# A Mamba mixer, cross attention and experts on one core: Delta's store, the load of B and C, w, the split of the products by C, and the order of the pieces

## The reference, cut to what matters

```python
h = conv(xc) + conv_b;  u = silu(h)                # 512 inner channels, 3 taps
dlt, Bm, Cm = split(u @ W_x.T)                     # 64, 16, 16
delta = softplus(dlt @ W_dt.T + b_dt)
dA  = exp(einsum('bld,dn->bldn', delta, -exp(A_log)))
dBu = einsum('bld,bln,bld->bldn', delta, Bm, u)
# scan in chunks of 64 tokens, the state starts at zero in each:
carry = dA * carry + dBu;  y = einsum('bkdn,bkn->bkd', carry, C)
y = y * silu(res);  out = y @ W_out.T + b_out
```

## Time and profile before

| | us |
|---|---|
| median of 3 runs (2793.26 to 2803.66) | 2795.64 |
| the profiled execution | 2792.28 |
| its span | 2790.5 |
| busy: PE | 2424.6 (87%) |
| busy: DVE | 2140.0 (77%) |
| busy: POOL | 2074.5 (74%) |
| busy: ACT | 1802.9 (65%) |

### The profile page before, as it was taken

How to read it: one execution, slowest core, us unless ns; L and a number is a source line. 1 busy time by engine, 2 the same in 40 slices (tenths; PEclk the granted TensorE clock), 3 DMA queues, 4 the chain that set the end, 5 groups by cost and what they waited for, 6 DMA issues and landing times. The chain is left out here.

```text
span 2790.5 us, 49779 instructions
## 1 busy us (share of the span) xinstructions
PE 2424.6 (87%) x14816; PEld 1660.6 (60%) x14816; DVE 2140.0 (77%) x3586; ACT 1802.9 (65%) x3972; POOL 2074.5 (74%) x968
## 2 busy tenths in 40 slices
PE   3578888888889898889889888898888879999998
PEld 2345666666666666666666666666665545555554
DVE  1778999999999999999999999999999832322332
ACT  1666777877888888777877787878777541211111
POOL 2999999999999999999999999999999500000000
PEclk8788999999999999999999999999998879999999
DMA  3456566666666666666666666666666360343221
GB/s 118 128 133 149 150 165 168 165 158 157 157 169 166 160 158 165 165 162 168 166 169 164 162 164 166 165 173 163 166 172 158 86 180 12 91 126 96 78 79 31
DMA packets 319323, 399.65 MB, mean 143 GB/s; under 512 B 115697, under 2 KB 256241, under 8 KB 314962
## 3 DMA queue, kind: packets, MB, share of 16 engines
q1 hardware_dynamic: 303698, 384.91, 53.5%
q10 hardware_dynamic: 15360, 11.55, 1.5%
HBM read 300.86 MB, written 94.37 MB: 142 GB/s over the span
## 5 line engine op out<-in xcount | busy, mean ns | idle before, releaser
L506 POOL TENSOR_TENSOR arena<-arena 128x1024 f32<-128x1024 f32 x512 | 1208.2, 2363 | 66.6 <-DMA arena<-w_dram 42.3
L582 ACT ACTIVATE dA_ps<-arena,a_neg 128x252 f32<-128x252 f32 x2048 | 868.7, 461 | 330.4 <-DVE dA_ps L787 172.0
L764 DVE TENSOR_TENSOR_SCAN arena<-dA_ps,arena 128x512 f32<-128x512 f32 x672 | 803.6, 1208 | 112.5 <-ACT dA_ps L582 88.0
L516 POOL TENSOR_TENSOR arena<-arena 128x1024 f32<-128x1024 f32 (+1 forms) x416 | 808.1, 1943 | 17.8 <-DVE arena L764 17.2
L764 DVE TENSOR_TENSOR_SCAN dA_ps<-dA_ps,arena 128x512 f32<-128x512 f32 x352 | 416.2, 1205 | 3.9 <-POOL arena L506 3.7
L887 PE MATMUL a_ps<-xT,w_conv 128*128 128x256 f32 x1536 | 369.8, 391 | 0.0
L829 DVE TENSOR_REDUCE mx<-s_ps 128x2 f32<-128x512 f32 x497 | 334.0, 672 | 23.2 <-PE s_ps L887 23.2
L887 PEld LDWEIGHTS a_ps<-xT,w_conv 128*128 128x128 f32 x1536 | 288.4, 194 | 54.1 <-issue 16.5
L887 PE MATMUL y_ps<-arena,sel 128*32 128x256 f32 x4096 | 257.5, 393 | 55.5 <-DVE m_rows L835 27.8
L640 ACT ACTIVATE probs<-st_ps 128x512 f32<-128x512 f32 x493 | 285.3, 579 | 29.7 <-PE st_ps L887 25.5
L887 PE MATMUL s_ps<-k_st,q_st 96*128 96x256 f32 x994 | 260.6, 344 | 43.7 <-DVE mx L829 28.0
(11 more groups left out here) (111 smaller groups left out, 3272.9 us busy)
## 6 DMA issues: line engine op xcount, KB each, us to landing
arena<-delta_dram SPq DMA_DIRECT2D x512, 128.0 KB, 2.8
arena<-w_dram SPq DMA_DIRECT2D x512, 128.0 KB, 3.2
arena<-bc_dram SPq DMA_DIRECT2D x128, 256.0 KB, 4.5
q_st<-q_parts_dram SPq DMA_DIRECT2D x512, 64.0 KB
k_st<-k_parts_dram SPq DMA_DIRECT2D x512, 64.0 KB
w_dram<-u SPq DMA_DIRECT2D x32, 512.0 KB, 2.8
delta_dram<-delta SPq DMA_DIRECT2D x32, 512.0 KB, 3.8
k_parts_dram<-parts SPq DMA_DIRECT2D x32, 512.0 KB, 4.0
```

What stands on the lines that cost most here:

```text
L506: pool.tensor_tensor(dBu[:, n % NB], w_r[:, n // RP % 2, t % RP].unsqueeze(1).to_broadcast([P, QS, L]), bc_r[:, b.par, 0], ALU.mult).then_ ...
L516: pool.tensor_tensor(h[:, n % NH, states], h[:, n % NH, states], bc_r[:, b.par, 1, states], ALU.mult).then_inc(s_hC, 1)
L582: last = nc.scalar.activation(dA[n % NDA][:, q, :, 1:], delta_r[:, n // (2 * RP) % 2, t % RP].rearrange("p (c t) -> p c t", t=CH)[:, :, 1: ...
L764: nc.vector.tensor_tensor_scan(dst, decays, dBu[:, n % NB, 2 * half:2 * half + 2].rearrange("p q t -> p (q t)"), 0.0, ALU.mult, ALU.add).t ...
```

## The change

- HC_DVE loses (1,0), (5,1) and (10,1) and gains (3,1) and (8,1): ten halves over nine tiles, where eleven lay over eight. The product by C on POOL has 7 whole tiles and 8 halves, where it had 8 and 5.
- On SP delta_store goes from offset 12 to 11, bc_load from 11 to 10 (behind replicate(3), ahead of load_stack(3)), w_store from 12 to 13 (behind load_ctx), replicate(1) from 19 to 18, store_x2T and the last columns from 97 to 99; the experts' first weights go a slot later, their tokens a slot sooner.
- On POOL w_piece goes from 12 to 13, behind dBu 13.
- On ACT xp_evac goes from 10 to 9, and the order within slots changes (the evacuation of q ahead of the decays, bc_store ahead of others). On DVE gating and q's subtraction stand ahead of the products by C, on PE x2T's transpose goes a slot sooner, and the order within slots changes.
- At the start the bias parts are loaded ahead of the convolution's weights; w_x, w_dt and w_gate have a semaphore of their own, for which x_proj waits; the other seven follow and the first state_sum waits for them. Batch 0's gate projection, evacuation and SiLU come behind its softplus. ACT makes the rounded copy of the bias rows.

```diff
-HC_DVE = [(1, 0), (1, 1), (4, 1), (5, 0), (5, 1), (6, 1), (8, 0), (9, 1), (10, 0), (10, 1), (14, 1)]
+HC_DVE = [(1, 1), (3, 1), (4, 1), (5, 0), (6, 1), (8, 0), (8, 1), (9, 1), (10, 0), (14, 1)]
@@ SP, start
+            for tile, name in bias_parts:
+                sp.dma_start(tile, io[name]).then_inc(s_bias_ld, 16)
             sp.dma_start(w_xc.rearrange("p q t -> p (q t)"), io["w_xc"]).then_inc(s_conv_ld, 16)
             sp.dma_start(conv_rows, io["conv_rows"].partition_broadcast(P)).then_inc(s_conv_ld, 16)
-            for tile, name in bias_parts:
-                sp.dma_start(tile, io[name]).then_inc(s_bias_ld, 16)
             def load_weights():
+                for tile, name in front_weights:
+                    sp.dma_start(tile, io[name]).then_inc(s_front, 16)
+                sp.wait_ge(s_const_v, N_SET)
                 for tile, name in weights:
                     sp.dma_start(tile, io[name]).then_inc(s_const, 16)
-                    sp.wait_ge(s_const_v, N_SET)
                 sp.wait_ge(s_const_p, 4)
@@ SP, the list
                 (O_K - 2, load_ctx),
+                (O_LD + 22, load_tokens),
+                (0 + 1, load_x),
+                (O_REP + 13, replicate(3)),
+                (O_REP + 5, replicate(1)),
...
                 (O_Q + 3, store_parts(q_dram, s_q_hi, s_q_lo, s_q_dram)),
...
+                (O_SP + 3, w_store),
+                (O_SP + 1, delta_store),
+                (O_XP + 1, bc_load),
                 (O_REP + 1, replicate(0)),
                 *[(O_LD + HG * gr - 2, load_stack(gr)) for gr in range(NG)],
+                (O_X2T + 5, store_x2T),
@@ POOL, the list
-                (O_SP + 2, w_piece),
+                (O_SP + 3, w_piece),
@@ ACT, new pieces
+            def silu_gate(b):
+                act.wait_ge(s_gate, b.value(2, 2))
+                nc.scalar.activation(gate[:, b.par], gate[:, b.par], ACT.Silu).then_inc(s_gsilu, 1)
             def silu(b):
                 act.wait_ge(s_conv, b.value(2, 2))
                 nc.scalar.activation(u[:], u[:], ACT.Silu).then_inc(s_u, 1)
+                if b.back(1):
+                    silu_gate(b)
                 nc.scalar.preload_act_table_set(EXP_LN)
+            def first_gate(b):
+                if not b.back(1):
+                    for half in range(2):
+                        gate_evac(half)(b)
+                    silu_gate(b)
+                    nc.scalar.preload_act_table_set(EXP_LN)
@@ ACT, the list
+                (O_SP + 2, first_gate),
+                (O_XP + 1, bc_store),
+                (O_XP, xp_evac),
@@ DVE, the list
                 *[(O_SCAN + t, scan(t, 1)) for t in range(NU)],
+                (O_Q + 1, low(s_q_hi, s_q_lo)),
+                *[(O_SCAN + 4 * m + 6, gating(m)) for m in range(ND)],
                 *[(O_SCAN + t, hC_piece(t, half)) for t, half in HC_DVE],
@@ PE
             def x_proj(b):
+                if not b.back(1):
+                    pe.wait_ge(s_front, 16 * len(front_weights))
+                    pe.wait_ge(s_const_v, N_SET)
                 pe.wait_ge(s_u, b.value(1, 1))
...
+                (O_X2T - 1, transpose(x_of, s_x2, TT, s_x2T_mm, s_x2T, bank_a, a_ps)),
+                (O_SP + 1, first_gate),
```

More of the change, by code:

```diff
@@ L530, in _ @@
             act.wait_ge(s_bias_ld, 16 * len(bias_parts))
+            act.wait_ge(s_const_v, N_ROWS)
+            nc.scalar.activation(bias[:], rows, ACT.Copy).then_inc(s_const_a, 1)
             nc.scalar.activation(a_neg[:], a_neg[:], ACT.Exp).then_inc(s_const_a, 1)
@@ L551, in silu, with later_gate_evac, piece @@
                 nc.scalar.activation(u[:], u[:], ACT.Silu).then_inc(s_u, 1)
-                act.wait_ge(s_gate, b.value(2, 2))
-                nc.scalar.activation(gate[:, b.par], gate[:, b.par], ACT.Silu).then_inc(s_gsilu, 1)
+                if b.back(1):
+                    silu_gate(b)
                 nc.scalar.preload_act_table_set(EXP_LN)
+            def first_gate(b):
[4 more added lines that the diff above has]
+                    nc.scalar.preload_act_table_set(EXP_LN)
+            def later_gate_evac(half):
+                def piece(b):
+                    if b.back(1):
+                        gate_evac(half)(b)
+                return piece
             def xp_evac(b):
@@ L701, in _ @@
                 (O_SP + 1, softplus),
+                *[(O_GATE + 4 * half + 2, later_gate_evac(half)) for half in range(2)],
+                (O_SILU, silu),
+                (O_SP + 2, first_gate),
+                (O_K + 1, high(s_k_mm, s_k_hi, s_q_dram, 1)),
+                (O_Q + 1, high(s_q_mm, s_q_hi, s_k_dram, 0)),
+                (O_N2 + 3, store_x2),
                 (O_V + 1, v_evac),
[L703 to L706, removed]
                 *[(O_SCAN + t - 1, decay(t, 0)) for t in range(NU)],
@@ L918, in gate_proj, with first_gate, later_gate, piece @@
                 return piece
+            def first_gate(b):
+                if not b.back(1):
+                    for m in range(ND):
+                        gate_proj(m)(b)
+            def later_gate(m):
+                def piece(b):
+                    if b.back(1):
+                        gate_proj(m)(b)
+                return piece
             def x_proj(b):
+                if not b.back(1):
+                    pe.wait_ge(s_front, 16 * len(front_weights))
+                    pe.wait_ge(s_const_v, N_SET)
                 pe.wait_ge(s_u, b.value(1, 1))
@@ L940, in piece @@
                     n = b.value(NU, 4 * m)
+                    if m == 0 and not b.back(1):
+                        pe.wait_ge(s_const, 16 * N_WEIGHTS)
+                        pe.wait_ge(s_const_p, 4)
                     pe.wait_ge(s_hC, b.value(len(HC_POOL), sum(t < 4 * m + 4 for t in HC_POOL)))
```

59 lines of the change are left out of this document (21 added, 38 removed).

## The result

| | before | after |
|---|---|---|
| median, us | 2794.45 (2792.62 to 2803.66, 4 runs) | 2839.76 (2837.34 to 2843.91, 4 runs) |
| the profiled execution's span | 2790.5 | 2840.3 |
| first dBu of batch 0 at | 70.65 | 54.30 |
| first dBu of batch 31 at | 2137.4 | 2183.1 |
| from there to the end | 653.1 | 657.2 |

The ratio is 1.0159, with a 95% interval of 1.0139 to 1.0179: slower by 1.6%. Of the 49.8 us between the spans the start gives back 16.3, the 31 periods cost 62.0 (68.67 in place of 66.67 us each) and the tail 4.1. So the loss is in the steady part.

The account below looks back on a forecast made before the run. The prediction took a serial cycle through softplus, context load and copies of w as the bound. It summed 2792.3 + 25 (steady batches) - 18 (start) = 2799, forecasting a 2803 us median, range 2765 to 2840.

Parts of the forecast that it names:

- What bounds the kernel: Steady batches: a serial cycle from first dBu through softplus, context load and copies, 66.85 us, with POOL's work at 64.5.
- Softplus at 48.0: Each batch: softplus ends 48.0 us after the first dBu instead of 48.65, as ACT's run starts 0.65 earlier.
- DVE's relief: Products by C: tile 5 keeps one half on DVE instead of two, bringing softplus 0.65 us forward.
- The sign named beforehand: POOL's waits: for the copies up from 0.9 to about 1.8 us a batch, on DVE near nothing.
- The base of the sum: Steady period: new sum of 67.7 us set against the measured 66.85, giving +0.8 a batch.
- From softplus to the next first dBu: End of batch: context load 7.2 us, w's store 0.56 later, landing 3.2, then 0.1, copies 8.6.
- The load of B and C: SP, slot 10 ahead of load_stack(3): costs nothing to 1 us of PE, under the wait for the copies.
- Delta's store: SP, behind load_stack(3): issued at about 1052, no sooner than 1051.77 despite its slot; landing off the path.
- Reordered pieces at nothing: Gating, q's subtraction, replicate(1), x2T's transpose and x_proj's evacuation moved earlier: costed at nothing; replicate(1) might remove 0.1.
- the rival of 2821: Steady batches: POOL's idle time stays 2.3 us and its work grows by 1.39, giving 2821; chance 0.10.
- The start: Batch 0: first dBu at about 52.5 us rather than 70.65, gain 18, from 10 to 19.
- the new chain at its full length: Steady batches: softplus stays 48.65 and copies take 9.4, so the period is 69.1 and the time 2848; chance 0.24.

Follow-up runs that it names:

- e8_w_bc_back: The changed kernel with w multiplied and stored in slot 12 again and the load of B and C a slot later as before: 2751.94 us, ratio 0.9856.
- e1: The changed kernel with w multiplied and stored in slot 12 again, all else as changed: 2766.68 us, ratio 0.9912.
- e7: The changed kernel with w in slot 12 again and the old eleven halves by C on DVE: 2775.54 us, ratio 0.9940.
- e9_best_stack0_late: e8_w_bc_back with one added wait on SP, so load_stack(0) goes out only after dBu of tile 15: 2787.18 us, ratio 0.9983.
- e5_ctx_behind: The changed kernel with the context load behind w's store on SP, w still multiplied a slot late: 2769.43 us, ratio 0.9931.
- e4_start_only: The kernel before with the new start alone; lists, halves and w as before: 2782.11 us, ratio 0.9960.
- e11: The kernel before with w a slot late and DVE's new order: 2881.01 us, ratio 1.0315.
- e12: The kernel before with w a slot late, the new start and ACT's and PE's new orders: 2857.51 us, ratio 1.0232.
- e2: The changed kernel with the old eleven halves by C on DVE, all else as changed: 2846.03 us, ratio 1.0194.
- e3: The kernel before with w multiplied and stored a slot later, nothing else: 2904.23 us, ratio 1.0402.

## Why the prediction was right in its range and wrong in its size

The median came out 37 us above the forecast of 2803 and on the same side of the kernel before, which the forecast had put 0.25% away and which is 1.6% away; "slower" had been given 0.36. It lies inside the range (2765 to 2840) by 0.24 us, where single runs of this kernel are 6.6 apart: that is luck, and one step of the working was wrong.

- **What bounds the kernel.** Right: a serial circle of softplus, context load, w's store, copies and first dBu, with POOL's work just under it. e8_w_bc_back shows both sides: with the circle shortened the period falls to 65.9, of which POOL works 65.5. That it would go no lower with a still shorter circle was not tried.
- **Softplus at 48.0: the step that failed.** It measured 49.4. This 1.4, less 0.2 in the rest of the circle, is 1.2 a batch or 37 us in 31 batches. The profiled execution lies 43 us above its own forecast of 2799; the other 6 are the start (2) and the tail (4), and the median doesn't show them because it lies 2.4 under the profiled execution rather than 3.4 over it. DVE's relief was right (47.9 in e1, 47.8 in e8, 0.7 less than with the old split in e7). In the ten batches whose convolution ran at full clock softplus comes at 47.9, as forecast; the other 13 make the difference. What the sum lacked is who stands behind replicate(0) on SP. I named load_stack(0) only as a neighbour that crowds the copies. Its nine transfers go out when replicate(0) has, and replicate(0) now waits for w's landing; PE waits for their rows, in 13 of 23 batches it then works at half clock, ACT waits for its transposed scores, and softplus stands at the end. e9_best_stack0_late shows this step by itself: load_stack(0) late and nothing else in the chain late gives 49.5. That the half clock is what makes the late batches late is read from the traces, batch by batch; no run delayed the stack and kept the clock up. The sign named beforehand was there as well: POOL's wait for the copies is the forecast 1.8 (1.7), but its waits on DVE, which should have vanished, are 1.2.
- **The base of the sum.** The 48.65 was one batch's; the mean before is 49.17. The prediction's own terms for the kernel before are 48.65 + 7.2 + 1.1 + 9.4 = 66.35, 0.5 short of the 66.85 that 67.7 was then compared with. With the same terms on both sides the rise is 1.35 a batch, not 0.8, and the forecast 2820. The 0.5 was made up by the reordered pieces (below), which the sum had at nothing.
- **From softplus to the next first dBu.** Forecast 7.2 + 0.56 + 3.2 + 0.1 + 8.6 = 19.7, measured 19.48. The sum is right by luck of two errors: w's store landed in 4.2 rather than 3.2, and the copies took 7.6 from first issue to landing rather than 8.6. The store did go out 0.55 behind the context load. This part is the loss that I had seen coming, 1.8 over the kernel before, and e5_ctx_behind takes 1.1 of it away, and 1.25 of softplus's lateness, with one swap.
- **The size of a late stack.** Not proportional: at 14.2 to 14.5 after softplus (e1, e5) softplus still comes at 48, at 15.5 to 15.8 (e9, after) it comes 1.5 later. The half clock goes with it: 0 and 1 batches there, 10 and 13 here. A sum of means can't show that. No run moved the stack in small steps, so where the slack ends between 14.5 and 15.5 stays open.
- **The load of B and C.** Forecast nothing to 1 us of PE a batch under cover of the copies. PE's wait is 0.7 a batch (25.4 less 9.5 us over 22 batches, most of it at the last heads, as is 14.9 of the 52.6 us in the kernel after: a sign that the prediction had named as speaking against it), but not covered: 9 to 15 us in all, part of it through w's store landing later, which I hadn't linked to this edit.
- **Delta's store.** No sooner, as forecast (1133.04, 2.2 after softplus's end; 3.0 in the earlier trace rows, and 3.0 in the mean of both). It lands in 6.0 rather than 3.8, off the path.
- **Reordered pieces at nothing.** Wrong. With the queue in time, e8_w_bc_back is 30 us faster than e4_start_only, and the new split, 6 to 9 us, is the only other thing in it that isn't a reordering; softplus is at 48.64 in e7 with the old split, and at 49.17 before. So they are worth some 20 us, by difference, and 23 and 36 where w is late (e11, e12). They soften the damage without undoing it.
- **POOL's work (the rival of 2821).** Refuted for the kernel after by e2: 1.4 us less of it in a batch gained nothing, though DVE got one product more by the same edit. By the Trainium skill (Perfetto Trace Analysis, Identifying the Most-Contended Engine) the busiest engine is the one to relieve first; the traces agree on which engine that is, in both kernels, but relieving it didn't help where it was tried (e2, e7). Only in e8 is POOL's own work the period, and nearly in e1, where it works 1487 of 1500 us.
- **The start.** Forecast 18, measured 16.3: the first dBu is at 54.30, not 52.5. Start of the kernel after, ACT, SP and POOL:

```profile
29.80 0.60 ACT L545 ACTIVATE u<-a_ps 128x512 f32<-128x512 f32 x1 [6.02 <-PE a_ps L910]
...
43.06 0.34 SPq L376 DMA_DIRECT2D w_dram<-u  x1
...
47.77 1.71 SPq L391 DMA_DIRECT2D arena<-delta_dram  x4
...
49.27 1.28 ACT L572 ACT_TABLE_LOAD   x1
...
54.30 2.35 POOL L511 TENSOR_TENSOR arena<-arena 128x1024 f32<-128x1024 f32 x1 [11.26 <-DMA arena<-w_dram]
```

u is evacuated 1.1 sooner than forecast. w's store is issued at 43.06, 0.4 later than the forecast's 58.7 less 16, and lands 4.6 us later rather than 3.2, so that replicate(0) starts at 47.77: there the 1.8 went. The deferred gate work ends at 50.6, hidden, as forecast.
- **The rival that came nearest** is the new chain at its full length: 2848 worked out, from a period of 69.1. The time is 8 off, the reason only half: its copies of 9.4 and its softplus of 48.65 are both wrong, in opposite directions.

## What to carry to other kernels

When a wait is lengthened on a queue that works in order, list everything that stands behind it, not only the transfer that you follow, and ask of each who waits for it and how much slack it has; here the harm came from a group of transfers of another stage, by way of PE, which stood for them, then got half its clock and kept ACT waiting. Of two pieces in one slot, the one that waits for the later event should stand behind, unless something later needs it more: that swap was worth 70 us. And undo each part of a bundle by itself: here one part lost 73 us and another 9 to 15 while the rest gained, and without those two the kernel is faster than both.

## What the runs showed of the hardware that was not expected

A short stand of PE can cost more than itself. In the kernel after PE stands 1.5 to 2.5 us for a late load in 13 of 23 batches; soon after, the granted clock is 0.50, and a group of 12 matmuls that takes 2.86 us at full clock takes up to 5.49. In the runs the mean granted clock over the whole execution goes with it: 0.945 after, 0.955 before, 0.96 in e1 and e8, 0.93 in e3.

The same store of 512 KB takes 3.0 us from issue to landing when it goes out first, with Delta's 0.5 us behind it (before), 3.2 in e8, 2.8 us behind Delta's, 4.2 with the context load issued within 1 us of it, ahead (after) or behind (e5), and Delta's store some us ahead and 6.5 when the load of B and C, nine small transfers and Delta's store of the same size have gone out just ahead of it (e1, e7). Delta's own store goes from 3.8 to 6.0 in the same way. No run varied one of these neighbours alone, so which of them costs what stays open; but a landing time measured at one place in the order can't be carried to another.
